# Two short edits at the hand-over from self-attention to cross-attention: VectorE's shift before its last refining, GpSimd's bias and mask behind that norm

## What is computed

```
x = x + attn(layernorm(x), Wq, bq, Wk, bk, Wv, bv, Wo, bo, rel_key)   # causal, 16 heads of 8, relative bias
x = x + xattn(layernorm(x), ctx, Wq, Wk, Wv, Wp, bp, ln_g, ln_b)      # 77 context tokens an element,
                                                                      # q and k normed per head, softmax(q k) v
x = x + ffn(layernorm(x), gate_w, lb_bias, w1, w2, cfc, cproj)        # top 2 of 8 experts + a shared one

def _layernorm(x, axis=-1, eps=1e-05):
    m = jnp.mean(x, axis=axis, keepdims=True)
    v = jnp.var(x, axis=axis, keepdims=True)
    return (x - m) / jnp.sqrt(v + eps)
```

## Time and profile before

| | us |
|---|---|
| three runs | 509.81, 510.57, 510.81; median 510.57 |
| the profiled execution's own time | 512.07 |
| its span, first to last instruction | 510.3 |
| TensorE busy | 456.9 (90% of the span) |
| VectorE busy | 346.3 (68%) |
| ScalarE busy | 260.9 (51%) |
| GpSimd busy | 162.0 (32%) |

### The profile page before, as it was taken

The page is one execution under the profiler, slowest core; times in us unless marked ns, Lnnn a source line. Parts: engine busy times, 40 slices in busy tenths (PEclk is TensorE's granted clock), DMA queues, the critical chain, the costliest instruction groups (busy, mean ns, idle before and its releaser), DMA issues.

```text
span 510.3 us, 17222 instructions
## 1 busy us (share of the span) xinstructions
PE 456.9 (90%) x7304; PEld 277.3 (54%) x7304; DVE 346.3 (68%) x692; ACT 260.9 (51%) x779; POOL 162.0 (32%) x95
## 2 busy tenths in 40 slices
PE   0758999999999799999799999998798999998997
PEld 0444555655655555655665655653444444565765
DVE  4974787656986757877757886857438577557543
ACT  1223746756556556556435746634234456555553
POOL 7236556331460963350951350275000000001000
PEclk9999999999999899999799999999568999999999
DMA  8112000000000000000000000000000004312251
GB/s 280 55 55 65 6 22 23 13 15 23 25 23 3 23 14 14 24 23 3 22 4 23 3 3 3 3 3 1 2 0 1 2 0 167 137 50 102 86 166 42
DMA packets 17465, 19.49 MB, mean 38 GB/s; under 512 B 1659, under 2 KB 14575, under 8 KB 17263
## 3 DMA queue, kind: packets, MB, share of 16 engines
q1 hardware_dynamic: 17391, 18.41, 11.1%
HBM read 16.17 MB, written 2.16 MB: 36 GB/s over the span
## 4 chain that ended last, share of the span: by engine, by line
PE 68%; DVE 20%; issue 5%; ACT 4%; DMA 2%; POOL 1%; SPq 0%; DVEq 0%; ACTq 0%; POOLq 0%
PE psT L1411 14%; PE psS L1382 13%; PE psS L1392 8%; PE psOM L1351 8%; PE psT L1771 5%; PE psS L1754 4%; DVE neg_max L1037 3%; PE psS L1601 2%; DVE x_max L1012 2%; PE psT L1492 2%; PE psOM L1492 2%; PE psOM L1628 2%; ACT prob L651 2%; DVE stat L822 1%; DVE stat L823 1%
## 5 line engine op out<-in xcount | busy, mean ns | idle before, releaser
L651 ACT ACTIVATE prob<-psS,neg_max 128x208 f32<-128x208 f32 (+23 forms) x256 | 121.2, 479 | 73.7 <-DVE neg_max L1037 73.5
L1037 DVE TENSOR_REDUCE neg_max<-psS 128x2 f32<-128x672 f32 (+23 forms) x128 | 91.8, 717 | 64.2 <-PE psS L1392 63.2
L444 POOL TENSOR_TENSOR stat<-stat,pack_a_sb 128x4 f32<-128x4 f32 (+2 forms) x16 | 54.6, 3416 | 183.4 <-DVE stat L864 153.0
L1411 PE MATMUL psT<-pack_a_sb,prob 128*128 128x128 f32 (+4 forms) x640 | 98.1, 285 | 6.3 <-DVE pt_even L993 3.3
L1411 PEld LDWEIGHTS psT<-pack_a_sb,prob 128*128 128x128 f32 (+4 forms) x640 | 64.4, 132 | 48.5 <-issue 31.4
L1382 PE MATMUL psS<-k_v,q_both 64*32 64x336 f32 (+23 forms) x2048 | 88.3, 401 | 2.6 <-ACT prob L651 1.4
L1392 PE MATMUL psS<-rel_shifted,q_both 36*32 36x268 f32 (+16 forms) x2048 | 71.6, 338 | 0.0
L478 POOL TENSOR_TENSOR q_both<-qT,pack_a_sb 128x1024 f32<-128x1024 f32 x16 | 31.5, 1972 | 89.7 <-PE psS L1392 81.7
L651 ACT ACTIVATION_READ_ACCUMULATOR prob<-psS,neg_max 128x1 f32 x256 | 50.6, 198 | 0.0
L1392 PEld LDWEIGHTS psS<-rel_shifted,q_both 36*32 36x32 f32 x2048 | 37.1, 109 | 24.7 <-issue 17.6
L1771 PEld LDWEIGHTS psT<-pack_b_sb,prob 128*128 128x128 f32 x288 | 36.1, 191 | 18.6 <-DVE prob L1257 11.4
(11 more groups left out here) (166 smaller groups left out, 614.2 us busy)
## 6 DMA issues: line engine op xcount, KB each, us to landing
q_rep<-q_scratch SPq DMA_DIRECT2D x128, 32.0 KB
k_v<-w_scratch SPq DMA_DIRECT2D x8, 512.0 KB, 6.4
q_both<-w_scratch SPq DMA_DIRECT2D x8, 512.0 KB, 6.3
pack_b_sb<-pack_b_dram SPq DMA_DIRECT2D x1, 1641.5 KB, 9.7
X<-x_dram SPq DMA_DIRECT2D x4, 256.0 KB, 5.8
q_scratch<-qT SPq DMA_DIRECT2D x4, 256.0 KB, 2.0
out_dram<-X SPq DMA_DIRECT2D x4, 256.0 KB, 2.3
pack_a_sb<-pack_a_dram SPq DMA_DIRECT2D x1, 535.0 KB, 4.8
```

The source lines that it names most:

```text
L444: nc.gpsimd.tensor_tensor(st[:, 5, 0:groups], st[:, 2, 0:groups], ca["root"][0:parts, 0:groups], ALU.pow).then_inc(seeded, 1)
L651: ins = nc.scalar.activation(prob[:, s % 4, half, 0:wide], psS[:, 2 * (s % 2) + half, 0:wide], ACT.Exp, bias=neg_max[:, s % 2, half:half + 1],
L1037: v.tensor_reduce(neg_max[:, s % 2], psS[:, 2 * (s % 2):2 * (s % 2) + 2, 0:wide], AX_X, ALU.max, negate=True).then_inc(max_ready, 1)
L1411: ins = nc.tensor.transpose(psT[0:w, k % 2, at:at + T], prob[:, s % 4, half, j * T:j * T + w], ident)
```

## The change

`x_shift(1)` moves ahead of the last norm's `refine` and `ln_multiply` on VectorE, and GpSimd waits for `ln_done` to reach 2 * B before `prepare(3)`, and so before `mask_keys(3)` behind it.

```
@@ -557,6 +557,8 @@
             pool.wait_ge(psO_ready, PRO + BLOCKS)
             copy_values(0, 1)
             root_tokens(2 * B - 1)
+
+            pool.wait_ge(ln_done, 2 * B)
             prepare(B - 1)
             mask_keys(3)
             for b in range(B):
@@ -1189,9 +1191,9 @@
             x_max_half(1, 6)
             ln_variance()
             x_max_half(1, 7)
+            x_shift(1)
             refine(stat, TB, B - 1 + 2 * B)
             ln_multiply()
-            x_shift(1)
             dve.wait_ge(x_tokens_ready, 1)
             v.tensor_copy(xnT[:], psM).then_inc(x_tokens_read, 1)
             x_max_half(2, 0)
```

## The result

The changed kernel takes 502.25 us in the median of four runs (501.14 to 503.06), before 510.69 (509.81 to 511.73, four runs, the three shown ahead and one more). The ratio is 0.983, 95% interval 0.980 to 0.986. That is 8.4 us less, where 3.2 were forecast. The profiled execution takes 502.75 us of its own time, its span is 500.9 (before 512.07 and 510.3). An execution more than 1.5% above the fastest of its kernel is left out of every ratio given here, but stands in the medians and ranges.

What follows compares the result with a forecast made beforehand. The prediction took the TensorE and VectorE chain as the bound, with TensorE waiting 3.15 us for a late shift. 510.57 - 3.15 gave 507.4 us, 0.6% faster, other terms costing nothing; range 504.0 to 509.5.

Steps and rivals of the forecast that it cites:

- the held refining and who holds it: VectorE's refining ahead of the shift: instructions of 1.22 and 2.20 us held until GpSimd's end; freed, 0.17 each.
- who isn't held: VectorE instructions with a PSUM input, such as the copy L1196 across GpSimd's mask, go on unharmed; copies take 673 to 694 ns.
- the gap's 3.15 us: TensorE idle from 357.16 to 360.31, between L1601 and transposes L1590, waiting for the shift; the whole 3.15 us goes.
- either edit alone would do nearly all of it: Wait only: shift ends 0.15 us behind TensorE's readiness; swap only: L1675 starts 0.4 us late; together they lose neither.
- nothing behind waits for GpSimd's later bias and mask: GpSimd's bias and mask move to 357.9 to 361.4; readers come much later, slack about 30 us, cost nothing.
- I take it that the rise goes with the work, so that the 3.15 us stand: Clock's return after the half-clock stretch, 378.60 before, moves up with the work; saving stays 3.15 us.
- The half-clock stretch, foreseen at 20.7 us: Sign to look for in the changed trace: the half-clock stretch some 20.7 us long, no longer 23.9.
- is busy nearly without a break from 360.31 and still stays at 0.50 for 18 us: Argument against the sooner clock, from TensorE behind the gap: work alone doesn't bring the clock back at once.
- the clock comes back sooner: Rival: without the gap, the half-clock stretch ends earlier; 507.4 less 1 to 8 us, taken as 503.5; chance 0.16.

Runs made afterwards that it cites:

- e2_wait: The changed kernel's GpSimd wait alone, without the swap: the shift stays behind the refining; 501.94 us, ratio 0.978.
- e1_swap: The swap alone, without GpSimd's wait: the shift moves ahead of the refining, which still meets GpSimd's bias and mask; 501.82 us, ratio 0.978.
- e9_fill3twice: The kernel before with the score products x_scores(3) computed three times, the shift left late; 505.46 us, ratio 0.989.
- e4_fill: The kernel before with the four score products of x_scores(3) computed twice, the shift left late; 505.69 us, ratio 0.987.
- e10_gap7_fill3: The changed kernel with seven repeats of the norm's square ahead of the shift and x_scores(3) computed four times; 506.01 us, ratio 0.992.
- e5_gap5: The changed kernel with five repeats of the norm's square on VectorE ahead of the shift; 508.00 us, ratio 0.994.
- e3_gap7: The changed kernel with seven repeats of the norm's square on VectorE ahead of the shift; 508.74 us, ratio 0.995.
- e12_gap3: The changed kernel with three repeats of the norm's square on VectorE ahead of the shift; 505.03 us, ratio 0.989.

## Why the prediction was wrong

Right, step by step: the held refining and who holds it (1.22 us became 0.16 in e2_wait, where only GpSimd's two instructions moved); who isn't held (the copy across the mask, 0.69 us); the gap's 3.15 us (3.0 by the landmarks); that either edit alone would do nearly all of it (though in e1_swap's profile TensorE, at full clock, waits 1.92 us for the norm, where I had 0.4); that nothing behind waits for GpSimd's later bias and mask.

Wrong: the step "I take it that the rise goes with the work, so that the 3.15 us stand". The predicted range ended at 504.0; the time is 502.25. The forecast's sum had one term for the gap and none for the clock, and the clock was the larger: 5.8 us in the stretch of the change. The half-clock stretch, foreseen at 20.7 us, measured 3.4.

The reason behind the step is what failed. I held against an early return that TensorE "is busy nearly without a break from 360.31 and still stays at 0.50 for 18 us". That observation was made on a kernel with the gap. It says how long the clock stays low behind a gap; I used it as if it said how long it stays low without one. The runs separate the two: with the shift still late but work in the gap, the clock is back at 357.1 to 358.0 (e9_fill3twice, e4_fill, e10_gap7_fill3); with the shift late and the gap open, it stays low for 13.7 to 17.1 us (e5_gap5, e3_gap7) though VectorE and GpSimd don't meet. The rival "the clock comes back sooner" was the right one. It was given 0.16 and priced at 503.5, the gap and 3.9 us for the clock; its bounds of 1 to 8 us below the forecast hold the 5.2 us by which the time lies below it. The rule of the Trainium skill named beside it (TensorE: Matmul & The Clock Gate, "What's actually happening": activity releases the throttle) agrees with the filled kernels, where more work in the gap went with a clock back at 357.1 to 358.0. It doesn't account for the two half-clock stretches in the next paragraph.

What stays open: what in TensorE's work brings the clock back. In e12_gap3 TensorE was busy 12.43 of 13.60 us and at half clock all that time, and from 374.3 in e10_gap7_fill3 even 10.10 of 10.10:

```profile
374.30:384.40 10.10, 10.10 (x51) 5.90 (x44) 7.42 (x19) 2.36 (x2) 0.00 (x0) 0.50 0.01 2
```

That the gap left open, and not the lateness, brings the long stretch behind 355 is shown by the gaps of 1.8 us and more against the filled ones, in the profiles and in the clock over all executions (0.965 and 0.966 against 0.973 to 0.975). Why 0.73 us of gap goes with 13.6 us at half clock and 1.05 us with 6.8 is not. Nor is it shown what decides the falls further on, which come, move and go from kernel to kernel with and without the gap.

## What to carry to other kernels

When a change opens or closes a wait of TensorE near a place where the granted clock changes its level, price it twice: its own length, and the half-clock time behind it. Here a gap of 1.8 to 3.2 us cost about 6. Don't take the length of a half-clock stretch as a property of the work in it; look for what idle time lies in it or ahead of it, and if the change removes that, give the full-clock durations a large chance in the forecast. And a small VectorE instruction that takes over a microsecond and ends with a GpSimd instruction is held by it: move one of the two, and check that its place is empty.

## What the runs showed of the hardware that was not expected

A kernel that computes the same four products twice, with nothing else changed, is 1.3% faster (e4_fill, 505.69 us, ratio 0.987).

Half-clock time is dear but not at its full rate: the 350 to 400 stretch has a mean clock of 0.73 before and 0.93 after, 20 us more at half, and 5.8 us were lost to them, 0.3 us each. The kernel before tells the same by itself. Its 65 executions beside the experiments that the ratios count took 507.0 to 513.35 us at mean clocks of 0.970 to 0.950, and a straight line through them gives 0.28 us for each microsecond more at half clock.

Executions of one program differ in their clock, and their times go with it: e5_gap5 took 504.70 us at a mean clock of 0.969 and 509.93 at 0.956. Kernels less than 1% apart can here only be compared by many executions, and the clock of each should be read beside its time.
